# Dilated attention: the branches' weights on GpSimd over two slots, mixing and sums one slot later on VectorE

## The reference

```python
        scores = jnp.where(mask, scores, -jnp.inf)
        lse = jax.nn.logsumexp(scores, axis=-1)
        o = jnp.einsum('bhqk,bkhd->bqhd', jnp.exp(scores - lse[..., None]), vd)
...
    lse_all = jnp.stack(lses, 0)[..., None]
    m = lse_all.max(0)
    w = jnp.exp(lse_all - m)
    w = w / w.sum(0)
...
    out = sum((o * wi.astype(o.dtype) for o, wi in zip(outs, w)))
    out = out.transpose(0, 2, 1, 3).reshape(B, L, E)
    return out @ Wo.T + bo
```

## Time and profile before

| what | value |
| --- | --- |
| median of 3 runs | 826.72 us |
| their range | 823.61 to 829.61 us |
| the profiled execution | 827.62 us |
| its span, first to last instruction | 825.9 us |
| busy, share of the span | PE 79%, DVE 60%, ACT 52%, POOL 43% |
| mean granted TensorE clock | 0.881 of 2.4 GHz |

### The profile page before, as it was taken

One profiled execution on the slowest core, in us unless ns is written; L12 is line 12 of the kernel. 1 busy time (PEld: TensorE's weight loads), 2 busy tenths in 40 slices (PEclk: granted clock), 3 DMA queues, 4 the chain that ended last, 5 costly groups with the idle time before them and its releaser, 6 DMA issues. The chain is left out here.

```text
span 825.9 us, 14463 instructions
## 1 busy us (share of the span) xinstructions
PE 653.9 (79%) x4946; PEld 479.1 (58%) x4946; DVE 497.5 (60%) x1624; ACT 432.9 (52%) x829; POOL 354.7 (43%) x482
## 2 busy tenths in 40 slices
PE   2989999549999999999644687778787982179995
PEld 2777777328788777877512345555454551046774
DVE  0467665856666666664115567797776445867741
ACT  1354432227866876687121465567555636427652
POOL 2133335473563365354422442445344414534653
PEclk9999999859999999999875797799887897569998
DMA  6235214273563555342221121233120413503433
GB/s 198 79 112 166 69 53 154 90 207 111 107 161 99 108 136 153 93 91 33 33 70 33 50 81 45 71 90 105 53 61 10 128 52 121 181 27 71 90 54 38
DMA packets 73882, 76.08 MB, mean 92 GB/s; under 512 B 8037, under 2 KB 66449, under 8 KB 73553
## 3 DMA queue, kind: packets, MB, share of 16 engines
q1 hardware_dynamic: 61217, 59.32, 23.1%
q0 software_dynamic: 10928, 15.57, 11.3%
q10 hardware_dynamic: 1664, 0.27, 0.2%
HBM read 52.20 MB, written 22.94 MB: 91 GB/s over the span
## 5 line engine op out<-in xcount | busy, mean ns | idle before, releaser
L1977 DVE CUSTOM_DVE_ANT_0 c_sn<-c_ps_s,k_mask 128x128 f32<-128x128 f32 (+1 forms) x256 | 75.8, 352 | 57.3 <-PE c_ps_s L2115 57.2
L1756 POOL TENSOR_SCALAR_AFFINE_SELECT c_pr<-c_pr 128x512 f32<-128x512 f32 x64 | 43.3, 676 | 114.2 <-ACT c_pr L1855 113.2
L1398 PE MATMUL b_ps_y<-e_w2h,b_hh 128*128 128x256 f16 x320 | 87.4, 273 | 1.4 <-DVE b_yb L1312 0.6
L1398 PE MATMUL b_ps_y<-e_w2h,b_hl 128*128 128x256 f16 x320 | 87.3, 273 | 0.0
L1398 PE MATMUL b_ps_y<-e_w2l,b_hh 128*128 128x256 f16 x320 | 87.3, 273 | 0.0
L1281 DVE TENSOR_TENSOR b_hl<-b_h,b_hh 128x640 f16<-128x640 f32 x64 | 53.2, 832 | 47.5 <-ACT b_hh L1229 47.5
L1207 POOL DMA_INDIRECT res<-b_y,b_s_idx x40 | 65.3, 1631 | 37.7 <-ACT b_y L1246 27.4
L1193 POOL DMA_INDIRECT e_xg<-rows,e_g_idx x35 | 38.6, 1104 | 81.8 <-DVE e_g_idx L1322 71.2
L2143 PE MATMUL c_ps_v<-c_pr,k_vx 128*64 128x256 f32 (+1 forms) x512 | 64.3, 379 | 4.7 <-POOL c_pr L1756 4.0
L1855 ACT ACTIVATE c_pr<-c_ps_t 128x768 f32<-128x768 f32 x64 | 51.7, 808 | 15.8 <-PE c_ps_t L2129 15.8
L2115 PE MATMUL c_ps_s<-k_ks,c_qs 48*128 48x128 f16 (+1 forms) x256 | 24.9, 279 | 42.8 <-DVE c_mx L1977 27.5
(11 more groups left out here) (423 smaller groups left out, 1835.9 us busy)
## 6 DMA issues: line engine op xcount, KB each, us to landing
e_w<-in_L_ffn_W_dram SPq DMA_DIRECT2D x16, 1024.0 KB, 5.9
s_raw<-in_L_ffn_W_down_dram SPq DMA_DIRECT2D x8, 640.0 KB
k_ks<-kT SPq DMA_DIRECT2D x48, 64.0 KB, 2.8
c_qs<-q SPq DMA_DIRECT2D x48, 64.0 KB, 2.4
s_raw<-in_L_ffn_W_up_dram SPq DMA_DIRECT2D x4, 682.0 KB, 4.2
rows<-a_rows SPq DMA_DIRECT2D x8, 264.0 KB, 2.7
rows<-s_rows SPq DMA_DIRECT2D x8, 264.0 KB, 2.2
a_x_in<-in_x_dram SPq DMA_DIRECT2D x8, 256.0 KB, 3.3
```

What stands on the lines that cost most here:

```text
L1398: last = pe.matmul(ps_y[(j + CT) % 2][:, 0:D], a, b[:, f, :], start=(f == 0 and k == 0), stop=(f == FC - 1 and k == 2))
L1756: pool.affine_select(out=late, in_=late, compare_op=ALU.is_ge, fill=0.0, base=0, pattern=[[0, 2], [0, 2], [1, P]], channel_multiplier=-1). ...
L1977: dve.tensor_tensor_reduce(sn[r][:, a:b], ps_s[:, r, a:b], mask[:, a:b], -1.0, 3.0e38, ALU.add, ALU.min, mx[g % 2][:, q, r, j:j + 1]).then ...
```

## The change

The seven and three weight instructions leave VectorE, except the reciprocal. GpSimd makes them in twelve: six in slot 1 behind its cut (`weights_begun`: `prod`, `some_key`, `live`, `zl` and two additions in place of the reduction), six in slot 2 behind the next cut (`weights_ended`: `none`, `zs1`, `ne`, `an`, `al`, `aw`). VectorE's reciprocal moves to slot 2 behind the maxima and waits for `zs1`; GpSimd's `al` waits for the reciprocal. The mixing goes to slot 3 behind the maxima, the two sums to slot 4 behind the split of the maxima and ahead of the maxima of f, 0. GpSimd's `vx` goes from slots 1 and 2 to slots 3 and 4. From step 0 on the statistics of `xs` go from slot 4 to slot 1. TensorE, ScalarE and SyncE keep their instructions and their order.

```diff
--- before.py
+++ after.py
@@ -1579,6 +1579,9 @@
...
         zl = sb("zl", [P, 2 * H, BR])
+        some_key = sb("some_key", [P, 2 * H, BR])
+        none = sb("none", [P, 2 * H])
+        zs2 = sb("zs2", [P, 2 * H])
         zs = sb("zs", [P, 2 * H])
...
@@ -1620,6 +1623,7 @@
...
         s_acc = sem("acc")
+        s_some = sem("some"); s_none = sem("none"); s_zs2 = sem("zs2")
         s_em = sem("em"); s_prod = sem("prod"); s_live = sem("live"); s_zl = sem("zl")
...
@@ -1748,6 +1752,49 @@
...
+            everywhere = member[:].unsqueeze(1).to_broadcast([P, 2, H, BR])
+            def pairs(t):
+                return t[:].rearrange("p (q h) b -> p q h b", q=2)
+            def weights_begun(m):
+                zb = acc[m % 2][:, :, :, 0:BR * (HD + 1)].rearrange("p q h (b e) -> p q h b e", b=BR)[:, :, :, :, HD]
+                after(pool, s_acc, m, 0, GROUPS)
+                after(pool, s_em, m)
+                pool.tensor_tensor(pairs(prod), zb, em[:].unsqueeze(3).to_broadcast([P, 2, H, BR]), ALU.mult)\
+                    .then_inc(s_prod, 1)
+                after(pool, s_prod, m)
+                pool.tensor_scalar(some_key[:], prod[:], 1.0, 0.0, ALU.is_equal, ALU.is_equal).then_inc(s_some, 1)
+                after(pool, s_some, m)
+                after(pool, s_al, m, 1)
+                pool.tensor_tensor(pairs(live), pairs(some_key), everywhere, ALU.mult).then_inc(s_live, 1)
+                after(pool, s_live, m)
+                pool.tensor_tensor(pairs(zl), zb, pairs(live), ALU.mult).then_inc(s_zl, 1)
+                after(pool, s_zl, m)
+                pool.tensor_tensor(zs2[:], zl[:, :, 0], zl[:, :, 1], ALU.add).then_inc(s_zs2, 1)
+                after(pool, s_zs2, m)
+                pool.tensor_tensor(zs[:], zs2[:], zl[:, :, 2], ALU.add).then_inc(s_zs, 1)
+            def weights_ended(m):
+                after(pool, s_zs, m)
+                pool.tensor_scalar(none[:], zs[:], 0.0, None, ALU.is_equal).then_inc(s_none, 1)
+                after(pool, s_none, m)
+                after(pool, s_rz, m, 1)
+                pool.tensor_tensor(zs1[:], none[:], zs[:], ALU.add).then_inc(s_zs1, 1)
+                pool.tensor_tensor(ne[:], none[:], em[:].rearrange("p q h -> p (q h)"), ALU.mult).then_inc(s_ne, 1)
+                after(pool, s_ne, m)
+                pool.tensor_tensor(an[:], third[:], ne[:].unsqueeze(2).to_broadcast([P, 2 * H, BR]), ALU.mult)\
+                    .then_inc(s_an, 1)
+                after(pool, s_rz, m)
+                pool.tensor_tensor(al[:], live[:], rz[:].unsqueeze(2).to_broadcast([P, 2 * H, BR]), ALU.mult)\
+                    .then_inc(s_al, 1)
+                after(pool, s_al, m)
+                after(pool, s_an, m)
+                after(pool, s_mix, m, 1)
+                pool.tensor_tensor(aw[:], al[:], an[:], ALU.add).then_inc(s_aw, 1)
             def cut(n, j):
...
@@ -1770,8 +1817,12 @@
...
                                         s_mr3, s_nmr3)
-                    if p in (1, 2) and within(g):
-                        j = p - 1
+                    if p == 1 and within(m):
+                        weights_begun(m)
+                    if p == 2 and within(m):
+                        weights_ended(m)
+                    if p in (3, 4) and within(g):
+                        j = p - 3
                         landed_after(pool, s_ldv, g, 2)
...
@@ -1962,11 +2013,6 @@
...
-            everywhere = member[:].unsqueeze(1).to_broadcast([P, 2, H, BR])
-
-            def pairs(t):
-                return t[:].rearrange("p (q h) b -> p q h b", q=2)
-
             def maxima(g, j):
...
@@ -1996,6 +2042,13 @@
...
                             .then_inc(s_nmc, 1)
+                    if p == 4 and within(m):
+                        after(dve, s_mix, m)
+                        dve.tensor_tensor(mix2[:], mix[:, :, 0, :], mix[:, :, 1, :], ALU.add).then_inc(s_mix2, 1)
+                        after(dve, s_mix2, m)
+                        after(dve, s_pot, m, 1)
+                        dve.tensor_tensor(o[:].rearrange("p q (h d) -> p (q h) d", h=H), mix2[:],
+                                          mix[:, :, 2, :], ALU.add).then_inc(s_o, 1)
                     if p < 4 and within(g):
...
@@ -2015,57 +2068,22 @@
...
                         dve.reciprocal(lrec[:], lsum[:]).then_inc(s_lrec, 1)
-                    if p == 4 and within(e):
+                    if p == (1 if n >= 0 else 4) and within(e):
                         landed(dve, s_ldx, e)
...
                         v = m % 2
-                        zb = acc[v][:, :, :, 0:BR * (HD + 1)].rearrange("p q h (b e) -> p q h b e", b=BR)[:, :, :, :, HD]
-                        if p == 1:
-                            after(dve, s_acc, m, 0, GROUPS)
-                            after(dve, s_em, m)
-                            after(dve, s_live, m, 1)
-                            dve.tensor_tensor(pairs(prod), zb, em[:].unsqueeze(3).to_broadcast([P, 2, H, BR]),
-                                              ALU.mult).then_inc(s_prod, 1)
-                            after(dve, s_prod, m)
+                        if p == 2:
+                            after(dve, s_zs1, m)
                             after(dve, s_al, m, 1)
-                            dve.scalar_tensor_tensor(out=pairs(live), in0=pairs(prod), scalar=1.0, in1=everywhere,
-                                                     op0=ALU.not_equal, op1=ALU.mult).then_inc(s_live, 1)
-                            after(dve, s_live, m)
-                            dve.tensor_tensor(pairs(zl), zb, pairs(live), ALU.mult).then_inc(s_zl, 1)
-                            after(dve, s_zl, m)
-                            dve.tensor_reduce(zs[:], zl[:], AX_X, ALU.add).then_inc(s_zs, 1)
-                            after(dve, s_zs, m)
-                            dve.scalar_tensor_tensor(out=zs1[:], in0=zs[:], scalar=0.0, in1=zs[:], op0=ALU.is_equal,
-                                                     op1=ALU.add).then_inc(s_zs1, 1)
-                            dve.scalar_tensor_tensor(out=ne[:], in0=zs[:], scalar=0.0,
-                                                     in1=em[:].rearrange("p q h -> p (q h)"), op0=ALU.is_equal,
-                                                     op1=ALU.mult).then_inc(s_ne, 1)
-                            after(dve, s_zs1, m)
                             dve.reciprocal(rz[:], zs1[:]).then_inc(s_rz, 1)
-                        if p == 2:
-                            after(dve, s_ne, m)
-                            dve.tensor_tensor(an[:], third[:], ne[:].unsqueeze(2).to_broadcast([P, 2 * H, BR]),
-                                              ALU.mult).then_inc(s_an, 1)
-                            after(dve, s_rz, m)
-                            dve.tensor_tensor(al[:], live[:], rz[:].unsqueeze(2).to_broadcast([P, 2 * H, BR]),
-                                              ALU.mult).then_inc(s_al, 1)
-                            after(dve, s_al, m)
-                            after(dve, s_an, m)
-                            dve.tensor_tensor(aw[:], al[:], an[:], ALU.add).then_inc(s_aw, 1)
+                        if p == 3:
                             after(dve, s_aw, m)
...
                                 .then_inc(s_mix, 1)
-                        if p == 3:
-                            after(dve, s_mix, m)
-                            dve.tensor_tensor(mix2[:], mix[:, :, 0, :], mix[:, :, 1, :], ALU.add).then_inc(s_mix2, 1)
-                            after(dve, s_mix2, m)
-                            after(dve, s_pot, m, 1)
-                            dve.tensor_tensor(o[:].rearrange("p q (h d) -> p (q h) d", h=H), mix2[:],
-                                              mix[:, :, 2, :], ALU.add).then_inc(s_o, 1)
                         if p == 6:
...
```

## The result

The changed kernel takes 832.45 us (median of 20 runs, 828.11 to 839.43), the one before 827.08 (20 runs beside it, 821.62 to 831.46). The ratio is 1.0069, 95% interval 1.0049 to 1.009: 0.7% slower, inside the 1% named as the bound, but with the other sign than the forecast. The profiled execution takes 834.89 us.

The account below looks back on a forecast made before the run. The prediction took VectorE in slots 1 to 4 as the bound. Its terms, -3.55 us for six steps, +0.7 and +1.8 for the last two, sum to -1.05 from 826.72: 825.6, rounded 825.5 us; range 816 to 837.

Parts of the forecast that it names:

- What bounded the kernel: Inside a step, VectorE bounds slots 1 to 4 and the other engines wait; after the last step the chain is latency.
- GpSimd's chain: Twelve dependent GpSimd instructions in slots 1 and 2, mean 0.305 us: halves of 2.2 and 2.0 us a step.
- GpSimd against VectorE: The skill's factor of two would add 20 us over eight steps; no trace row confirmed it, so it was left out.
- Blocking: Slots 3 and 4: VectorE's split and sums wait for GpSimd instructions beside them; split done 0.95 us after the mixing.
- Gain of a whole step: 0.35 us: Steps with `le` and slot 4 maxima: output product at 559.1 instead of 559.47, so 0.35 us gained each.
- First and sixth step: First has no `le`: 0.7 us gained; sixth has no slot 4 maxima ahead of `lmx`: 1.1 us more gained.
- Step seven: No maxima, so VectorE was not the bound; `o` comes later behind the half chains: 0.7 us lost.
- Step eight: Nothing hides the chain; first weight to mixing grows from 2.5 to 4.3 us: 1.8 us lost.
- light blocking: Rival, chance 0.25: engines hardly block each other in slots 3 and 4; 8.5 us gained, 818.2 us.
- The swallowed gain: Rival, chance 0.10: gain lost behind slot 4 to ScalarE's order or scores; last two steps lose 2.5 us, 829.2 us.
- The longer chain: Rival, chance 0.20: GpSimd instructions average 0.43 us, 1.5 us more in each of eight steps; +12 us, 837.5 us.

Follow-up runs that it names:

- e14: e12 plus eight filler matmuls on TensorE in slot 4 of every step with weights and maxima; ratio to the kernel before 1.0006.
- e10: Changed kernel plus ten filler matmuls on TensorE in step eight, between the router's logits and the transposition of the sums; ratio to the kernel before 1.0123.
- e1: Changed kernel with weights, mixing and sums of steps seven and eight back on VectorE in slots 1 to 3; 827.89 us, ratio to the kernel before 0.9997.
- e6: Changed kernel with one more instruction, a copy of the two-operation comparison, in the second half of GpSimd's chain; ratio to the kernel before 1.0193.
- e5: Changed kernel with VectorE's split of the maxima moved from slot 4 to slot 3, ahead of the mixing; ratio to the kernel before 1.0114.
- e12: Changed kernel without the fourth instruction of GpSimd's chain (product with the heads' membership), so weights differ from the reference's; ratio to the kernel before 1.0049.
- e11: Changed kernel with value copies in slots 5 and 6, router's maximum before sums, split before mixing, last two steps' weights on VectorE; ratio to the kernel before 0.9958.
- e13: Changed kernel plus eight filler matmuls on TensorE in slot 4 of every step with weights and maxima; ratio to the kernel before 1.0034.

## Why the prediction was wrong

- **What bounded the kernel**: right for the waits (the scores' wait went from 17.6 to 1.5 us), wrong for the end of a step. VectorE's slots 1 to 4 reach the step's end only through `le` and `xn`: over the split and ScalarE's copies in before, over `lmx` in after.
- **GpSimd's chain**: the straight line between the rows gave 0.305 us an instruction; measured 0.348. The additions of 32 elements fit (0.24 to 0.26 against 0.245), the products of 96 roughly (0.36 to 0.43 against 0.36, 0.16 us over the six together); the two-operation comparison is half of the miss of 0.5 us, 0.556 against 0.30. The line was drawn through products alone, and the trace of before had rows that do not lie on it: a product of 16 elements with a scalar at 0.336 us (L1792), a power taken of 2 elements at 0.717 (L1744). So `aw` came 5.3 us behind slot 1's cut, not 4.8, and VectorE idled 2.38 us at the reciprocal, not 1.7.
- **GpSimd against VectorE**: the Trainium skill's factor of two ("GPSIMD Engine Reference", section 4.1), which the prediction set aside, is not what these rows show at this size: 0.36 to 0.43 us on GpSimd for the six products of 96 elements, 0.20 to 0.33 on VectorE for the same six in step eight of before, a factor of 1.25 to 1.8, in sum 1.4.
- **Blocking**: right. From the mixing's end to the split 0.9 us (forecast 0.95), sums 1.16 and 0.77 (1.05 and 0.80).
- **"Gain of a whole step: 0.35 us"** is the step that failed. It was read from the output product, 559.1 against 559.47, while the same paragraph had `le` no earlier, 557.85 against 557.79. A step follows `le` and `xn`, so by the forecast's own numbers its gain was nil. e14, with the chain about as long as forecast and the clock held up, measures just that: `le` 13.86 and a step of 27.06, as before. With the chain as it is the third and fourth step lost 0.46 us each; with the clock as it falls, steps two to five lost 1.9 us together (1.1 in e10) instead of gaining 1.4. This is one half of the miss; the sizes of the last two steps (3.3 us as well) are the other.
- **First and sixth step**: forecast -0.7 and -1.45, measured -0.96 and -2.06, but +0.09 and -1.18 in e10 with the same code, so single profiles neither bear these terms out nor refute them.
- **Step seven**: forecast +0.7, measured +2.2 (+1.0 in e10); e1 gives all of it back, and part of it is the clock: the output product took 2.87 us in after and 1.89 in e10.
- **Step eight**: forecast +1.8, measured +3.6. `em` to mixing grew by 2.4 (from 2.80 to 5.22), and 1.0 came from TensorE's clock, which no term had (e10).
- **The rivals**: light blocking did not occur. The swallowed gain is the closest: by ScalarE's order a step gains nothing (e14), 829.2, with the chain and the last two steps mis-sized. The longer chain had the right price by length in e6 (0.62 of 0.63 us), at a mean of 0.348 where it put the break-even at 0.33.

Sum against the forecast: 3.3 from steps two to five, -0.9 from one and six, 1.5 and 1.8 from the last two, 5.7 us, which is 4.67 + 1.05. How it falls on the first seven steps is uncertain by about a microsecond each: e10 takes 177.8 us for them as after does, but its terms are 2.5, 1.1 and 0.3.

## What to carry to other kernels

Before pricing a gain, follow it to what the next repeat of the loop waits for, and check that this very instruction moves; a product that starts sooner and is not waited for is no gain. A wait that is long in the profile may cost nothing (e5 moved the largest one by 2 us for no change) while a short new one, 0.7 us at `le`, marks the path. Look what runs beside an instruction before moving it to another engine: changing the place of the copies alone gave more than moving the work.

## What was not expected of the hardware

- On GpSimd a comparison with two operations on 96 elements takes 0.556 us, a product of two inputs of that size 0.36 to 0.43.
- How long TensorE's clock stays down does not follow the wait before it. In the third step it stood at the lower level, 1.2 GHz, for 3.4 us in before, 6.8 in after and 10.2 in e12 and in e11, with waits in slot 4 of 1.2, 2.7, 2.5 and 1.2 us; in e12 it fell within the wait, in after shortly before its end, and in e10, with the code of after, it fell 2.4 us sooner and ahead of that wait. The output product took 1.9 us or up to 3.0. Eight filler matmuls in that slot held the clock at 2.4 GHz in the third step (e13, e14), but in e13's second step it had fallen before they began.
